# Four attention layers on one core: the second layer's projections moved into the first layer's last steps

## The reference, cut to what matters

```
score = einsum('bndi,bndj->bnij', rq, k) * SCALE
prob = softmax(score); attn_vec = einsum('bnij,bndj->bndi', prob, v)
attn_out = einsum('od,bdl->bol', Wo, attn_vec) + bo
x = attn_out + z1ss
return (x - m) * rsqrt(var + LN_EPS)
```

```
q = hidden_state @ Wq + bq;  k = encoder_hidden_state @ Wk + bk;  v = encoder_hidden_state @ Wv + bv
scores = einsum('bkgld,bksd->bkgls', q, k) * scale + encoder_attention_mask
out = einsum('bkgls,bksd->bkgld', softmax(scores), v)
x = out @ Wo + bo + hidden_state
```

## Time and profile before

| what | us |
|---|---|
| median of 3 runs (lowest, highest) | 1301.92 (1301.35, 1302.68) |
| the profiled execution | 1302.4 |
| its span in the profile | 1300.6 |
| PE, DVE, ACT, POOL busy | 1235.3, 817.5, 751.0, 574.2 |
| layer 0's last step ends | about 380 |
| first scores of layer 1 | 401.50 |

### The profile page before, as it was taken

How to read it: one execution, slowest core, us unless ns; L and a number is a source line. 1 busy time by engine, 2 the same in 40 slices (tenths; PEclk the granted TensorE clock), 3 DMA queues, 4 the chain that set the end, 5 groups by cost and what they waited for, 6 DMA issues and landing times.

```text
span 1300.6 us, 24533 instructions
## 1 busy us (share of the span) xinstructions
PE 1235.3 (95%) x8912; PEld 1016.2 (78%) x8912; DVE 817.5 (63%) x1840; ACT 751.0 (58%) x2026; POOL 574.2 (44%) x607
## 2 busy tenths in 40 slices
PE   6999999999987997999999999999999898999799
PEld 5777777777744555889999988999999675878687
DVE  3666666866647995666666776666667514788610
ACT  4765666566545885655555555555554433888842
POOL 3665554556339984150302131322120314899710
PEclk9999999999998999999999999999999999999999
DMA  7101111010010003120202020202000100100000
GB/s 270 52 28 33 49 47 34 27 54 27 5 68 1 1 2 126 38 58 25 74 10 74 9 74 10 74 10 74 10 17 2 67 1 1 66 1 2 1 9 25
DMA packets 15525, 50.44 MB, mean 39 GB/s; under 512 B 1840, under 2 KB 5296, under 8 KB 14384
## 3 DMA queue, kind: packets, MB, share of 16 engines
q1 hardware_dynamic: 15408, 48.87, 11.1%
HBM read 47.82 MB, written 1.05 MB: 38 GB/s over the span
## 4 chain that ended last, share of the span: by engine, by line
PE 79%; DVE 8%; POOL 6%; ACT 5%; issue 2%; DMA 1%; SPq 0%; DVEq 0%; ACTq 0%; POOLq 0%
PE pS L1534 13%; PE pT L1562 7%; PE acc L1614 6%; PE acc L326 6%; PE pC L406 5%; PE pT L393 5%; PE pS L376 4%; PE pS L1576 4%; PE pC L1599 4%; PE acc L362 3%; PE heads_scores L1344 3%; PE heads_scores L1355 3%; POOL probs L2447 2%; PE pT L1587 2%; DVE stats L1248 2%
## 5 line engine op out<-in xcount | busy, mean ns | idle before, releaser
L1534 PE MATMUL pS<-split_sources,split_pair_weights 128*128 128x512 f32 x768 | 212.0, 411 | 5.8 <-issue 4.3
L722 POOL TENSOR_TENSOR probs<-probs,stats 128x512 f32<-128x512 f32 x128 | 130.4, 1040 | 140.1 <-DVE stats L587 140.1
L528 ACT ACTIVATE probs<-pS,stats 128x256 f32<-128x256 f32 x256 | 117.8, 472 | 102.1 <-DVE stats L582 102.1
L1711 ACT ACTIVATE probsT<-pT 128x256 f32<-128x256 f32 x128 | 49.1, 384 | 197.1 <-PE pT L1587 197.1
L1534 PEld LDWEIGHTS pS<-split_sources,split_pair_weights 128*128 128x128 f32 x768 | 135.9, 190 | 30.7 <-issue 6.6
L1614 PE MATMUL acc<-l_wo_parts,l_ctx_parts 128*128 128x256 f32 x768 | 121.9, 295 | 1.0 <-DVE l_ctx_parts L1783 1.0
L1562 PEld LDWEIGHTS pT<-l_wv_parts,split_sources 128*128 128x128 f32 x756 | 106.9, 188 | 14.2 <-issue 2.2
L1837 POOL TENSOR_TENSOR split_pair_weights<-weights_a,split_pair_weights 128x1024 fp32r<-128x1024 f32 x16 | 38.0, 2379 | 170.1 <-ACT split_pair_weights L1675 170.0
L1562 PE MATMUL pT<-l_wv_parts,split_sources 128*128 128x256 f32 x756 | 110.6, 281 | 2.1 <-issue 2.1
L1614 PEld LDWEIGHTS acc<-l_wo_parts,l_ctx_parts 128*128 128x128 f32 x768 | 99.4, 190 | 1.2 <-DVE l_ctx_parts L1783 1.2
L326 PE MATMUL acc<-split_sources,split_pair_weights 128*128 128x512 f32 x372 | 99.5, 402 | 0.8 <-POOL split_pair_weights L704 0.7
(11 more groups left out here) (254 smaller groups left out, 2883.5 us busy)
## 6 DMA issues: line engine op xcount, KB each, us to landing
weights_a<-in_l_w SPq DMA_DIRECT2D x16, 768.5 KB, 4.2
weights_a<-in_l_w SPq DMA_DIRECT2D x16, 768.0 KB, 5.9
value_bias_rows<-in_l_bv SPq DMA_DIRECT2D x16, 256.0 KB, 4.4
weights_b<-in_l_wo SPq DMA_DIRECT2D x16, 256.0 KB, 2.6
w_fc<-in_l_w SPq DMA_DIRECT2D x4, 1024.0 KB, 5.9
bias_rows<-in_rows SPq DMA_DIRECT2D x1, 1536.0 KB, 13.5
x_residual<-in_x_dbl SPq DMA_DIRECT2D x2, 512.0 KB, 7.1
masked_scores<-in_ctx_dbl SPq DMA_DIRECT2D x2, 512.0 KB, 8.1
```

The source lines that it names most:

```text
L528: a = e.activation(self.E[:, n % 4, h, it, :], self.S[h][:, it, :], ACT.Exp, bias=self.st[:, 1, n % 4, h, it:it + 1], accum_out=self.st[:, ...
L722: e.tensor_tensor(self.E[:, n % 4, h, :, :], self.E[:, n % 4, h, :, :], self.st[:, 3, n % 4, h, :].unsqueeze(2).broadcast_to([P, 2, D]), A ...
L1534: mm = e.matmul(bank[:, :], self.w_qk[i % 2][kw][:, 1 - which, c, h * P:h * P + P], g.split[:, which, ks, c, half * HALF:half * HALF + HAL ...
```

## The change

What it does:

- Layer 1's first four projections (keys and queries of the first half of the tokens) are issued in steps 60 to 63 of layer 0, its values (now 64 columns in place of 128, all batches in one bank, one evacuation) in step 64. The split of the context goes to steps 60 to 64, the split of layer 2's first weights to steps 66 and 67, and their loads wait for less.
- The other four projections go into steps 1, 2, 4 and 5 of layer 1's loop, in bank `pC`, through `claim`.
- The sum of batches 4 to 7 is transposed just before the loop and in step 0, its statistics and normalisation go to DVE's steps 0 to 3, `rstd` to POOL's units 1 and 2, and the back-transposes to PE's and ACT's steps 7, 9, 11 and 13 (bank `pC`, through `claim`).
- The output bias is added by a matmul of the identity with the bias rows, ahead of the two of the output projection. POOL's eight adds are gone.
- Queries and keys swap their buffers, and the second buffer of transposed probabilities is `w2` in place of `hT`.

```diff
@@ Layer0.pe, step n (act, dve and pool likewise)
+            self.next.pe_ahead(e, n - self.N + 4)
             if 0 <= n - 4 < self.N:
                 output(n - 4)
...
-        for b in range(4, B):
-            sum_transposes(b)
...
     def back_bank(self, b):
-        return (self.g.pT, self.g.pC)[b % 2] if b >= 4 else self.bV
+        return self.g.pC if b >= 4 else self.bV
@@ Project
+    def pe_values(self, e):
+        g = self.g
+        wait(e, self.qk, 3)
         for b in range(B):
...
             for c in range(KC):
+                mm = e.matmul(self.v_bank[:, 64 * b:64 * b + 64], g.cT[:, c, b * P:b * P + P],
+                              self.wv[:, c, 0:64], start=c == 0, stop=c == KC - 1)
+        mm.then_inc(self.v_full.sem, 1)
+
+    def pe_ahead(self, e, n):
+        if 0 <= n < 4:
+            self.pe_group(e, n)
+        if n == 4:
+            self.pe_values(e)
...
+    def act_ahead(self, e, n):
+        cross, split = self.cross, self.split
+        if 0 <= n < 2:
+            self.act_group(e, n)
+        if n == 3:
+            self.act_group(e, 2)
+            self.act_group(e, 3)
+        if 0 <= n < 4:
+            split.high(e, n)
+        if n in (6, 7):
+            cross.high_qk(e, n - 6, 0)
+            cross.high_qk(e, n - 6, 1)
+        if n == 7:
+            cross.high_v(e, 0)
+            cross.high_v(e, 1)
...
+    def dve_ahead(self, e, n):
+        if 1 <= n < 5:
+            self.split.low(e, n - 1)
+        if n == 5:
+            self.dve_values(e)
@@ SmallHeads.pool
-        for b in range(B):
-            e.tensor_tensor(g.x[:, b, :], g.x[:, b, :], self.bo, ALU.add).then_inc(self.xb.sem, 1)
...
+            if r in (1, 2):
+                self.l0.rstd(e, r + 1)
@@ SmallHeads.pe
         def output(b):
             claim((self.x, b + 1))
+            e.matmul(self.bX[:, 0:D], g.ident, self.bo, start=True, stop=False)
             for c in range(KC):
...
+        def rows_of_first_layer(b):
+            claim((l0.x_done, b + 1))
+            l0.back_transposes(e, b)
...
+            if t in (1, 2, 4, 5):
+                n = t + 3 - (t >= 4)
+                claim((project.qk, n + 1))
+                project.pe_group(e, n)
...
+            if t in (7, 9, 11, 13):
+                rows_of_first_layer(4 + (t - 7) // 2)
@@ SmallHeads.act
+            if t in (1, 2, 4, 5):
+                self.project.act_group(e, t + 3 - (t >= 4))
             if 0 <= t - 1 < self.R:
                 exps(t - 1, 0)
+            if t in (7, 9, 11, 13):
+                self.l0.evacuate_x(e, 4 + (t - 7) // 2)
@@ SmallHeads.dve
+            if t < 2:
+                self.l0.stats(e, 4 + 2 * t)
+                self.l0.stats(e, 5 + 2 * t)
+            elif t < 4:
+                self.l0.normalise_h(e, 2 * t)
+                self.l0.normalise_h(e, 2 * t + 1)
```

More of the change, by code:

```diff
@@ L562, in act @@
                     self.evacuate_x(e, b)
-        for b in range(4, B):
-            self.raw(e, b)
     def raw(self, e, b):
@@ L928, in sp @@
-    def sp(self, e):
-        pass
-    def project(self, e, which):
-        n = 4 * which
-        for half in range(2):
-            if half == 1 and not (self.keys_ahead and which == 0):
-                for sem, value in self.prev:
-                    wait(e, sem, value)
-            for m in range(2):
-                if n >= 4:
-                    wait(e, self.qk, n - 3)
-                for c in range(KC):
-                    mm = e.matmul(self.banks[n % 4][:, :], self.ws[which][:, c, m * P:m * P + P],
-                                  self.srcs[which][:, c, half * HALF:half * HALF + HALF],
-                                  start=c == 0, stop=c == KC - 1)
-                mm.then_inc(self.full.sem, 1)
-                n += 1
@@ new lines, in half, with pe_group @@
+    @staticmethod
+    def half(h):
+        return slice(h * HALF, h * HALF + HALF)
+    def pe_group(self, e, n):
+        g, l0 = self.g, self.l0
+        kind, k = self.order[n]
+        h, m = divmod(k, 2)
+        w, src = (self.wk, g.cT) if kind == "k" else (self.wq, g.hT)
+        if n == 0:
+            for sem, value in self.w_loaded:
+                wait(e, sem, value)
+            e.wait_ge(l0.qk_lo, l0.N)
+        elif n == 1:
+            e.wait_ge(l0.v_ready, l0.v_step(l0.N))
+            e.wait_ge(l0.f_raw, 4)
+            e.wait_ge(l0.x_done, 4)
+        elif n < 4:
+            wait(e, self.qk, n - 1)
+        if kind == "q":
+            e.wait_ge(l0.h_done, 4 * (h + 1))
+        for c in range(KC):
+            mm = e.matmul(self.banks[n][:, :], w[:, c, m * P:m * P + P], src[:, c, self.half(h)],
+                          start=c == 0, stop=c == KC - 1)
+        mm.then_inc(self.full.sem, 1)
@@ L955, in pe @@
+    def pe_values(self, e):
+        g = self.g
+        wait(e, self.qk, 3)
         for b in range(B):
-            if b < 4:
-                wait(e, self.qk, 5 + b)
-            else:
-                wait(e, self.vs, b - 3)
             for c in range(KC):
-                mm = e.matmul(self.banks[b % 4][:, 0:width], self.kv_src[:, c, b * P:b * P + P],
-                              self.wv[:, c, :], start=c == 0, stop=c == KC - 1)
-            mm.then_inc(self.full.sem, 1)
-    def evacuate(self, e, which):
-        n, dst = 4 * which, (self.kT, self.qT)[which]
-        for half in range(2):
-            for m in range(2):
-                wait(e, self.full, n + 1)
-                ts = slice(half * HALF, half * HALF + HALF)
-                i = e.activation(dst[:, m, ts], self.banks[n % 4][:, :], ACT.Identity,
-                                 bias=self.bs[which][:, m:m + 1])
-                i.then_inc(self.qk.sem, 1)
-                n += 1
@@ new lines, in pe_values, with act_group @@
+        mm.then_inc(self.v_full.sem, 1)
[4 more added lines that the diff above has]
+            self.pe_values(e)
+    def act_group(self, e, n):
+        kind, k = self.order[n]
+        h, m = divmod(k, 2)
+        dst, bias = (self.kT, self.bk) if kind == "k" else (self.qT, self.bq)
+        if n == 0:
+            e.wait_ge(self.l0.rest_loaded, 48)
+            e.wait_ge(self.l0.s_full, self.l0.N - 4)
+        elif n == 2:
+            e.wait_ge(self.l0.s_full, self.l0.N)
+        wait(e, self.full, n + 1)
+        e.activation(dst[:, m, self.half(h)], self.banks[n][:, :], ACT.Identity, bias=bias[:, m:m + 1])\
+            .then_inc(self.qk.sem, 1)
@@ L1104, in scores @@
                 wait(e, self.scaled, r)
+            else:
+                wait(e, l0.f_x, B)
+                wait(e, project.qk, 4)
+            if b == 4:
+                wait(e, project.qk, 7 + m)
             wait(e, self.keys, r + 1)
@@ L1117, in transposes @@
                 wait(e, self.pt1, r)
+            else:
+                wait(e, l0.f_raw, B)
             for k in range(8):
```

299 lines of the change are left out of this document (126 added, 173 removed).

## The result

| what | before | changed |
|---|---|---|
| median, us (lowest, highest; 7 runs each) | 1301.92 (1301.35, 1303.26) | 1306.94 (1304.05, 1307.88) |
| ratio to before, 95% interval | 1 | 1.0028 (1.0018 to 1.0039) |
| the profiled execution | 1302.4 | 1307.88 |
| its span | 1300.6 | 1306.1 |
| first scale and mask of layer 1 | 402.77 | 386.70 |

A second series of the changed kernel, beside the second set of experiments, gave 1306.24 (1305.61 to 1308.37, 9 runs), ratio 1.0035 (1.0023 to 1.0048). The change costs 0.3 to 0.4%. The forecast was 1302.2 with a range up to 1306.5: the first median lies 4.7 us above the forecast and 0.4 above the range, that of the second series 0.3 inside it.

A forecast was written before the change was run, and what follows sets the result against it. Layer 1's steady state was taken as four engines nearly full, with PE alone bounding the gap between layers. Terms -15.5 + 4.6 + 3.8 + 3.5 + 3.9 = +0.3 us gave 1302.2, range 1296.0 to 1306.5.

The forecast's parts named there:

- Groups in steps 60 to 63: Layer 0's last steps: PE bounds each step at 5.10 us in place of 4.57, 2.1 us in all.
- Rival C: Layer 0's last steps don't absorb the four groups, which cost 6.9 us rather than 2.1: 1307.0; chance 0.12.
- Values and start: Step 64: values take 3.5 us, step grows about 3.1; layer 1's first scale and mask at 387.3, 15.5 us earlier.
- DVE in steps 0 to 3: Layer 1's first steps: statistics and normalisation add to DVE, the bound there, with nothing covering them: +4.6 us.
- Groups 6 and 7 by the claim: Layer 1's steps 4 and 5: waits around the shared bank make loops of 6.9 us for 5.01, +3.8 us.
- Rival B: Layer 1's thin start runs partly at 1.2 GHz, costing 1.9 to 3.9 us: 1304.2 to 1306.1; chance 0.16.
- Rows in steps 7 to 13: Layer 1's steps 7, 9, 11, 13: transposes and a 0.8 us wait for ACT's copy delay PE, +3.5 us.
- The bias: Identity matmul ahead of layer 1's output projection: 0.49 us in each of eight batches, +3.9 us.
- Rival A: The shared bank costs little in layer 1, so 3.8 + 3.5 us go: 1294.9; chance 0.28.

The follow-up runs named there:

- values32: Changed kernel with only 32 of the 64 value columns per batch projected, half the values left out; 1308.71 us, one run.
- pool_waits: Changed kernel with one more wait: in unit 3 POOL starts its mask and shifts only once the last rows are normalised; 1300.24 us, ratio 0.9989 to before.
- norm_one_port: Changed kernel, batches 6 and 7 normalised by a tensor_scalar with accumulator, product with reciprocal deviation left out; 1300.94 us, ratio 0.9989 to before.

## Why the prediction was right and wrong

**Groups in steps 60 to 63: right.** Steps of 5.09 against 5.10. Rival C, that they don't fit there, is excluded.

**Values and start: right.** 3.52 against 3.5, step 64 at 6.04 against 6.1, first scale and mask at 386.70 against 387.3. The load's pitch held down to 32 columns (values32). The start was worth 16.1 us and not 15.5: from the end of the last residual add to the scale and mask it took 1.34 us and not 1.7.

**DVE in steps 0 to 3: the step that failed.** The prediction said "the normalisation of two batches 1.11, in steps 2 and 3", priced by a row from between the layers, where POOL ran only instructions on 128x4 tiles. In step 3 POOL's key mask and four shifts run beside it, and the same four operations took 4.08. Without that (pool_waits, norm_one_port) the stretch is +3.7, under the +4.6 I gave, mostly because DVE had waited 0.61 us for unit 3's scores before the change and the added work fills that wait; with it +6.7. The trace of before had a warning that I didn't read. Between its layers, `split_sources` took 1.2 us an operation while POOL added biases, and in the changed kernel, in layer 0's steps, the same operation's median is 0.684. The timeline of the kernel before:

```profile
391.66 4.69 DVE L903 TENSOR_TENSOR split_sources<-ctxT,split_sources 128x512 fp32r<-128x512 f32 x4 [6.07 <-ACT split_sources L895]
```

```profile
391.67 7.32 POOL L1078 TENSOR_TENSOR x_residual<-x_residual,bias_rows 128x256 f32<-128x256 f32 x8
```

And the normalise itself had an instance of 1359 ns among its 16, in layer 0's own steps, beside an instruction of 1.28 us of POOL (L704 at 250.54), by the view of its line (count, then min/median/max in ns), where I had read only the groups' means:

```profile
L692 DVE TENSOR_SCALAR hT<-hT,stats x16: 331/341/1359, 237.5 to 385.3; 128x128 f32<-128x128 f32 x16
```

**Groups 6 and 7 by the claim: mechanism and size right, the clock missed.** Predicted +3.8; with the clock at full speed +4.0 (pool_waits), in the changed kernel +5.8 and in its repeat +6.9. The loop of 6.9 us per step is there: from the scale and mask of unit 5 to that of unit 6 it is 428.48 - 421.61 = 6.87. Rival B named the clock, in scores, transposes and groups, and expected "up to 3.9 if it reaches steps 4 and 5". Its sign, a clock under 0.8 in the thin start, is in both profiles: 0.74 from 390 to 395 in the first series and 0.73 from 395 to 400 in the repeat. But that stretch cost DVE nothing, as the room of 2 us that B allowed held (unit 0 to 4 takes 25.94 and 25.95). What did cost time was a second low stretch in step 4, 1.8 us and 2.9 in the repeat, behind the idle time that the stretched normalise made. It came behind 2.70 us of idle PE too, without the stretch. So B happened in part, and its price was paid at a place and behind a wait that I had not seen.

**Rows in steps 7 to 13: mechanism right, too large.** The wait is 0.75, predicted 0.8; but PE's loop is late by 0.59 each, not 0.9: more of it is hidden. That makes 2.4 us against 3.5 (4 x 0.9 would have been 3.6).

**The bias: right, a little large.** 0.43 each against 0.49, 3.4 against 3.9 us. Together these two were expected at +7.4 and measured at +6.3.

**Rival A** (the shared bank costs little) is refuted: periods of 11.86, loops of 6.87.

**The sum.** The terms that I had, with their measured sizes, make a gain: -16.1 + 3.7 + 4.0 + 6.3 = -2.1. The two I hadn't, 2.9 for the stretch and 1.8 for the clock, bring it to +2.6, the account's +2.7. Those that I had came out 2.4 us below my +0.3, mostly DVE's and the rows' terms, which I had priced too high. That this hid half of the 4.7 us that I had missed is luck. The medians stood 5.0 us apart in the first series and 3.6 in the second, where the copy came 2.7 and 3.4 us late. Some of it is layer 3's clock, which was low in different executions of every kernel; how the rest divides stays open. The "no change" that I forecast was a small difference of large terms, so a missed 4.7 us decided its sign. The range's top of 1306.5 took in rival B's 1306.1 and left C's 1307.0 out; no case had two small losses together. At the other end the range is misread in the prediction: A's own time, 1294.9, lies below 1296.0, so it doesn't take in most of A.

## What to carry to other kernels

Price an operation by a row from a place where the other engines do what they will do at its new place. When DVE work moves into a loop in which POOL is always busy, look for the longest instance of that operation in the trace, not only its mean: 1.36 against 0.34 us for one normalise operation was there before the change. If DVE then stands still at POOL's pace, let POOL wait for the few short operations (a wait of 1.24 us gave back 2.9 of stretch and, with the clock and layers behind, 6.0 of the median). A form that reads one tensor with an accumulator passed too, but here it left out a product. And behind a new idle time of PE, work the sum out at either clock, as no run here shows when exactly it falls. Compare profiles of two kernels only after looking whether PE went the same way in both.

## What the runs showed of the hardware that I had not expected

- DVE operations on 128x128 tiles take 1.0 us each instead of 0.34 or less when POOL runs 1.0 us instructions beside them, in two forms (`tensor_scalar` with two scalars, 4.08 for four; `scalar_tensor_tensor` with two SBUF inputs, 4.20). A `tensor_scalar` with an accumulator took 1.14 for four under the same POOL work, and DVE's scale and mask, whose scores come from PSUM, stays at 2.28 beside it as well. Beside POOL's instructions on 128x4 tiles the first form took 1.11 for four. POOL kept its own pace beside it: four shifts took 4.03 in the changed kernel and in pool_waits.
- A projection group fell to 1.2 GHz (3.78 us for 1.99) after 5.63 us of idle PE and also (3.68) after 2.70 us, but not after 1.11 (1.99) or 0.66 (1.99). The length of the idle time doesn't settle it, though: after 1.90 us the scores of unit 1 took 2.02 us in one execution of the changed kernel and 1.14 in another.
- Matmuls with a 128-column load keep a pitch of 0.11 us with 64 and with 32 moving columns, and with 32, in the one run, the clock read 0.66 in the window right behind them.
